# Bias adds on GpSimd, denominators by transposes, and Kronecker inner products on 64x64 blocks with zeros

## What is computed

```python
# L0 and L3, MLP with two biases (the block before is an attention)
y = y + (gelu(norm(y) @ w1 + b1) @ w2 + b2)
# L2 cross-attention and L3 self-attention: softmax in two steps
o = exp(scores) @ v ; out = (o / sum(exp(scores))) @ Wo
# L0 feed-forward: each row goes to 2 of 64 experts, with weights s_k;
# an expert is a sum of Kronecker products, applied to the row as a 32x32 matrix X
h = gelu(sum_k s_k * (B_k.T @ (X @ A_k)) * scale + bias)
```

## Time and profile before

| | us |
|---|---|
| median of 3 runs | 3536.96 (3536.55 to 3546.62) |
| time of the profiled execution | 3511.47 |
| its span, in which all times of the trace are given | 3509.7 |
| PE busy in the span | 3134.8 (89%) |
| DVE, ACT, POOL busy | 1798.4, 1190.6, 958.8 |
| mean granted clock of PE | 0.948 of full speed |

### The profile page before, as it was taken

One profiled execution on the slowest core, in us unless ns is written; L12 is line 12 of the kernel. 1 busy time (PEld: TensorE's weight loads), 2 busy tenths in 40 slices (PEclk: granted clock), 3 DMA queues, 4 the chain that ended last, 5 costly groups with the idle time before them and its releaser, 6 DMA issues. The chain is left out here.

```text
span 3509.7 us, 74620 instructions
## 1 busy us (share of the span) xinstructions
PE 3134.8 (89%) x30164; PEld 2164.7 (62%) x30164; DVE 1798.4 (51%) x4511; ACT 1190.6 (34%) x2326; POOL 958.8 (27%) x794
## 2 busy tenths in 40 slices
PE   8997999999976868889778999789997999989989
PEld 3434555555666764757445555489997885566656
DVE  7897544543233554343676666543333763355543
ACT  1223333323223432312315565322222562244433
POOL 1002433432001100425427778411111210104001
PEclk9998999999989989979889999889998999999999
DMA  4223000000132020635501110178886200021100
GB/s 154 70 72 87 10 13 13 9 9 14 38 56 25 4 53 0 187 100 173 150 25 33 30 31 22 55 277 330 331 328 226 95 2 13 29 72 50 53 14 19
DMA packets 174053, 287.24 MB, mean 82 GB/s; under 512 B 79254, under 2 KB 144331, under 8 KB 164408
## 3 DMA queue, kind: packets, MB, share of 16 engines
q1 hardware_dynamic: 166264, 262.50, 23.8%
q0 software_dynamic: 7488, 20.46, 1.8%
HBM read 244.50 MB, written 28.48 MB: 78 GB/s over the span
## 5 line engine op out<-in xcount | busy, mean ns | idle before, releaser
L2708 PE MATMUL ps<-L_ffn_xsT,arena 128*128 128x128 f32 x2584 | 306.2, 278 | 0.9 <-DVE L_ffn_xsT L2507 0.9
L2708 PEld LDWEIGHTS ps<-L_ffn_xsT,arena 128*128 128x128 f32 x2584 | 298.9, 194 | 3.0 <-DVE L_ffn_xsT L2507 2.6
L842 POOL TENSOR_TENSOR L_xattn_rn<-L_xattn_ss,mhalf 125x16 f32<-125x16 f32 (+1 forms) x64 | 185.8, 2903 | 257.2 <-DVE L_xattn_ss L905 257.2
L162 POOL TENSOR_TENSOR rstd<-nsc,mhalf 112x4 f32<-112x4 f32 (+2 forms) x24 | 39.4, 1641 | 691.0 <-DVE nsc L155 690.1
L3389 POOL TENSOR_TENSOR L_xattn_pT<-L_xattn_pT,L_xattn_keep 125x678 int32<-125x678 int32 x128 | 190.4, 1510 | 70.2 <-ACT L_xattn_pT L3644 70.2
L2606 ACT ACTIVATE L_ffn_silu<-ps,arena 128x128 f32<-128x128 f32 x280 | 102.9, 368 | 269.3 <-PE ps L2708 253.5
L2516 DVE SCALAR_TENSOR_TENSOR L_ffn_hT<-ps,arena,L_ffn_silu 128x128 f32<-128x128 f32 x280 | 98.0, 351 | 155.9 <-ACT L_ffn_silu L2606 155.9
L2385 POOL DMA_INDIRECT L_ffn_rows_out<-L_ffn_ys,L_ffn_dest x78 | 79.8, 1023 | 319.7 <-DVE L_ffn_ys L2525 304.1
L1019 PE MATMUL ps<-arena,L_xattn_cT 128*125 128x512 f32 x384 | 166.1, 592 | 0.0
L723 PE MATMUL ps<-L_attn_prod,arena 128*32 128x448 f32 (+28 forms) x672 | 153.5, 492 | 11.6 <-DVE L_attn_prod L523 9.7
L2721 PE MATMUL ps<-arena,L_ffn_hT 128*128 128x256 f32 x646 | 153.7, 382 | 7.4 <-ACT L_ffn_ys L2615 7.3
(11 more groups left out here) (610 smaller groups left out, 6808.4 us busy)
## 6 DMA issues: line engine op xcount, KB each, us to landing
arena<-in_L_ffn_up SPq DMA_DIRECT2D x35, 2056.0 KB, 8.1
arena<-in_L_ffn_down SPq DMA_DIRECT2D x35, 1152.0 KB, 8.8
L_xattn_ctxT<-in_ctxT SPq DMA_DIRECT2D x48, 375.0 KB, 4.1
arena<-in_L_ffn_up SPq DMA_DIRECT2D x43, 384.0 KB, 4.7
L_attn_a<-L_attn_skew SPq DMA_DIRECT2D x16, 784.0 KB, 5.2
L_xattn_ctx<-in_ctx SPq DMA_DIRECT2D x30, 375.0 KB
arena<-L_xattn_kp SPq DMA_DIRECT2D x64, 93.8 KB, 3.3
L_xattn_mask<-in_mask SPq DMA_DIRECT2D x32, 164.1 KB, 8.3
```

Source lines behind the costliest of these rows:

```text
L842: nc.gpsimd.tensor_tensor(rn[0:r, i], ss[0:r, i], core.mhalf[0:r, 0:H], ALU.pow).then_inc(po_r.step("root", i), 1)
L2708: ins = nc.tensor.matmul(ps[:, 2 + b % 4, half * TS:(half + 1) * TS], self.up(i % WU, k, half * HM + m), xsT[:, i % 2, k], start=(k == 0), ...
```

## The change

Five edits, of which the last only feeds the others.

1. `Mlp`: b2 is loaded into 112 rows, POOL adds it to x, one chunk (112x1024) at a time, and PE's product with the ones is gone. POOL's loop over chunks is written out; the add of chunk c stands behind the power of chunk c + 1. DVE waits for it ahead of its first add to x.
2. `denominators` in `L2Cross` and `L3Self` are 4 transposes of a quarter of o. The 16 numbers stand 32 columns apart in PSUM, and DVE reads them there.
3. `L0Kron.inward` takes both experts at once: for each pair g and each r one product of 64x64 by 64x64, with X twice on the diagonal of the 64x64 input and zeros beside it.
4. The zeros are written by POOL before the loads. Each chunk has a buffer of its own: chunk 0 the second half of h (7168 numbers in each of 128 partitions), chunk 1 `y` (4096) and `xs` (3584). The load of chunk 0 waits for the first memset, that of chunk 1 for all three, and it no longer waits for u0.
5. The bias of L3's MLP is also made in 112 rows, in the stage ahead of it.

```diff
@@ L0Kron.build
+        by_g = lambda t, n: t[:, 0:n * K * I].rearrange("p (g m) -> p g m", g=n)
+        flat_y, flat_xs = core.y[:, :, :].rearrange("p b c -> p (b c)"), self.xs.rearrange("p g n -> p (g n)")
+        YG = NB * D // (K * I)
+        blocks = [[(0, CG, by_g(flat[:, CG * F:2 * CG * F], CG))],
+                  [(0, YG, by_g(flat_y, YG)), (YG, CG, by_g(flat_xs, CG - YG))]]
...
             def load(q):
                 src = x_rows.rearrange("(g r) (i n) -> r i g n", r=2, n=I)
-                for c in range(4):
-                    sp.dma_start(self.xs[c * I:(c + 1) * I], src[c // K][:, q * CG:(q + 1) * CG, :]).then_inc(rows_in[q], DMA)
+                sp.wait_ge(zeroed, 3 if q else 1)
+                for a, b, to in blocks[q]:
+                    for c in range(4):
+                        sp.dma_start(to[c * I:(c + 1) * I, :, c % K * I:(c % K + 1) * I], src[c // K][:, q * CG + a:q * CG + b, :]).then_inc(rows_in[q], DMA)
...
             load(0)
-            sp.wait_ge(pe_t.sem, pe_t.at(first["u0"] + INNER - 1))
             load(1)
...
         def _(pool):
             norm_pool(core, norm)
+            nc.gpsimd.memset(flat[:, CG * F:2 * CG * F], 0.0).then_inc(zeroed, 1)
+            nc.gpsimd.memset(flat_xs, 0.0).then_inc(zeroed, 1)
+            pool.wait_ge(pe_x.sem, pe_x.at(NCH - 1, "xT", KD - 1))
+            pool.wait_ge(rows_out, DMA)
+            nc.gpsimd.memset(flat_y, 0.0).then_inc(zeroed, 1)
...
             def inward(name, q):
...
-                            for c in range(4):
-                                p = slice(c * I, (c + 1) * I)
-                                ins = nc.tensor.matmul(ps[p, even(n) + b, s * F:(s + 1) * F], self.xs[p, g, :], table[p, g, :], start=True, stop=True)
+                            for r in range(2):
+                                p = slice(r * K * I, (r + 1) * K * I)
+                                ins = nc.tensor.matmul(ps[p, even(n) + b, s * F:(s + 1) * F], part[g][p], table[p, g, :], start=True, stop=True)
@@ Mlp.build
         def _(pool):
-            with pool.Fori(0, NCH) as c:
-                ln.pool(pool, ve_n, po, c)
+            ln.pool(pool, ve_n, po, 0)
+            pool.wait_ge(run.arrived, run.loads)
+            for c in range(NCH):
+                if c + 1 < NCH:
+                    ln.pool(pool, ve_n, po, c + 1)
+                x = core.x[0:T, U * c:U * c + U, :]
+                nc.gpsimd.tensor_tensor(x, x, self.b2.unsqueeze(1).to_broadcast([T, U, D]), ALU.add).then_inc(biased, 1)
...
             def outputs(c):
+                dve.wait_ge(biased, c + 1)
+                core.stand(dve)
...
-                                         start=(i == 0), stop=False)
-                    nc.tensor.matmul(ps[0:T, 4 + u, 0:D], core.ones[0:1, 0:T], self.b2, start=False, stop=True).then_inc(pe_o.step("out", u), 1)
+                                               start=(i == 0), stop=(i == HK - 1))
+                    ins.then_inc(pe_o.step("out", u), 1)
@@ L3Self.build (L2Cross alike, with 97 rows and columns in place of 128)
             def denominators(n):
...
-                    ins = nc.tensor.matmul(ps[0:T, 3, j * HQ:(j + 1) * HQ], o[:, n % 3, j * T:(j + 1) * T], core.ident[:, 0:128:Z], start=True, stop=True)
+                    ins = nc.tensor.transpose(ps[0:T, 3, j * 128:(j + 1) * 128], o[:, n % 3, j * T:(j + 1) * T], core.ident[:, :])
```

More of the change, by code:

```diff
@@ L1168, in build @@
         by_scalar = [first[name] + t for name, turns in self.ORDER if name[0] in "tabuwv" for t in range(turns)]
-        norm, lead, folded, rows_out = (core.semaphore(n) for n in ("norm", "lead", "folded", "rows_out"))
+        norm, lead, folded, rows_out, zeroed = (core.semaphore(n) for n in ("norm", "lead", "folded", "rows_out", "zeroed"))
         rows_in = [core.semaphore(f"rows_in{q}") for q in range(CHUNKS)]
@@ L1222, in _ @@
             norm_pool(core, norm)
+            nc.gpsimd.memset(flat[:, CG * F:2 * CG * F], 0.0).then_inc(zeroed, 1)
[3 more added lines that the diff above has]
+            nc.gpsimd.memset(flat_y, 0.0).then_inc(zeroed, 1)
             for q in range(CHUNKS):
+                if q == 0:
+                    pool.wait_ge(pe_t.sem, pe_t.at(first["u0"] + INNER - 1))
                 if q == 1:
-                    pool.wait_ge(rows_out, DMA)
                     pool.wait_ge(pe_t.sem, pe_t.at(first["u1"] + INNER - 1))
@@ L1574, in inward @@
                 table_kept(f"a_up{q}")
-                ten.wait_ge(rows_in[q], 4 * DMA)
+                ten.wait_ge(rows_in[q], 4 * len(blocks[q]) * DMA)
+                part = {g: to[:, g - a, :] for a, b, to in blocks[q] for g in range(a, b)}
                 for t in range(INNER):
@@ L1689, in build @@
         yn, yT, hT = sb("yn", [T, U, D]), sb("yT", [128, KD, N4]), sb("hT", [128, HK, N4])
-        ln, lead = Norm(core, run, "ln"), core.semaphore("lead")
+        ln, lead, biased = Norm(core, run, "ln"), core.semaphore("lead"), core.semaphore("biased")
         pe_t, pe_u, pe_o = Progress(core, "tensor_yT", ("yT", KD)), Progress(core, "tensor_up", ("up", HK)), Progress(core, "tensor_out", "out")
@@ L1799, in narrow @@
                             ten.wait_ge(ac_h.sem, ac_h.at(c, "act", i))
-                        nc.tensor.matmul(ps[0:T, 4 + u, 0:D], hT[:, i, u * T:(u + 1) * T], self.w2[:, i, :],
-                                         start=(i == 0), stop=False)
-                    nc.tensor.matmul(ps[0:T, 4 + u, 0:D], core.ones[0:1, 0:T], self.b2, start=False, stop=True).then_inc(pe_o.step("out", u), 1)
+                        ins = nc.tensor.matmul(ps[0:T, 4 + u, 0:D], hT[:, i, u * T:(u + 1) * T], self.w2[:, i, :],
+                                               start=(i == 0), stop=(i == HK - 1))
+                    ins.then_inc(pe_o.step("out", u), 1)
             turn(0, True)
@@ L1826, in weights @@
         self.b1 = a.load(d["L0_xattn_b1_c"], 128, self.HK)
-        self.b2 = a.load(every(d["L0_xattn_b2"], 1), 1, D)
+        self.b2 = a.load(every(d["L0_xattn_b2"], T), T, D)
         self.gain = a.load(d["L0_xattn_ln2_g_c"], 128, KD)
@@ L3297, in build @@
         sb, v, kT, k = run.sbuf, self.v, self.kT, self.k
+        DR = (HQ - 1) * Z + 1
         xn, xT = sb("xn", [T, 2, D]), sb("xT", [128, 2, KD * T])
@@ L3495, in inverses @@
                     dve.wait_ge(ac_r.sem, ac_r.at(n - 2, "wide"))
-                nc.vector.reciprocal(inverse[:, n % 2], ps[0:T, bank, at:at + H]).then_inc(ve_r.step("inverse"), 1)
+                nc.vector.reciprocal(inverse[:, n % 2].rearrange("p (j h) -> p j h", j=NQ), ps[0:T, bank, at:at + NQ * DR].rearrange("p (j r) -> p j r", j=NQ)[:, :, 0:DR:Z]).then_inc(ve_r.step("inverse"), 1)
             def divided(n, bank):
@@ L3780, in denominators @@
                 for j in range(NQ):
-                    ins = nc.tensor.matmul(ps[0:T, bank, at + j * HQ:at + (j + 1) * HQ], o[:, n % 2, j * T:(j + 1) * T], core.ident[:, 0:128:Z], start=True, stop=True)
+                    ins = nc.tensor.transpose(ps[0:T, bank, at + j * DR:at + (j + 1) * DR], o[0:DR, n % 2, j * T:(j + 1) * T], core.ident[0:DR, 0:DR])
                 ins.then_inc(pe_r.step("den"), 1)
@@ L4589, in inverses @@
                     dve.wait_ge(ac_r.sem, ac_r.at(n - 2, "wide"))
-                nc.vector.reciprocal(inverse[:, n % 2], ps[0:T, 3, 0:H]).then_inc(ve_r.step("inverse"), 1)
+                nc.vector.reciprocal(inverse[:, n % 2], ps[0:T, 3, 0:H * Z:Z]).then_inc(ve_r.step("inverse"), 1)
             def divided(n):
@@ L4929, in flat @@
             return v
-        row = lambda s: flat(s.rearrange("(a n) -> a n", a=1), 1, 0)
+        row = lambda s: flat(every(s, T), T, 0)
         later = lambda s: None
@@ L4938, in weights @@
         self.bf = generated(lambda s: flat(s, 128, 0), col_d_named(col_d, n + "cf"), n + "cf", lambda s: s, False, mix["cf", "b"])
-        self.bm = generated(row, d, n + "cm", lambda s: s, False, mix["cm", "b"][0:1, :])
+        self.bm = generated(row, d, n + "cm", lambda s: s, False, mix["cm", "b"][0:T, :])
         self.items = [self.cf, self.cm, self.bf, self.bm]
```

## The result

| | before | after |
|---|---|---|
| median of the runs | 3536.82 us (3536.55 to 3546.62) | 3476.10 us (3474.65 to 3479.65) |
| ratio | | 0.9823 (95%: 0.9805 to 0.9842) |
| profiled execution, its span | 3511.47, 3509.7 | 3474.65, 3472.8 |

The change takes off 60.7 us; forecast were 39.2, with 3484 to 3513 us as the range. The direction was right and the size was not. The two profiled spans are only 36.9 us apart, which looks like the forecast's sum and isn't: the first experiment shows why.

What follows compares the result with a forecast made beforehand. PE bounds the MLPs and L3's self-attention, its instruction supply the Kronecker inner products. -19.5 - 7 - 24 + 8.7 + 2.6 = -39.2 us, from 3536.96 to 3497.8 us, predicted as 3497.5; range 3484 to 3513 us.

Steps and rivals of the forecast that it cites:

- 4 chunks of 4 batches in two stages are 32 products of 0.61 us: Both MLPs: removing PE's bias products saves 19.5 us, all of it on the path.
- POOL's add and its cover: MLPs: POOL's add of b2 takes 2.4 us a chunk, under some 8 us of cover, cost 0.
- rival D: MLPs: POOL's add holds L254 and stops PE; at 14 us an add the kernel takes 3549 us; chance 0.02.
- 32 times 0.24: L2 cross-attention and L3 self-attention: denominators by transposes save 7.7 us, taken as -7 (bounds -3 and -9).
- Forecast 2 x 12.1: Kronecker stage: two inner products at 14.8 us in place of 26.9 save 24 us (bounds -21 and -26.6).
- The reading of the pause as want of instructions: Kronecker stage: PE pauses 1.81 us because instructions run out, 3.8 us for each 128 records whatever their shape.
- Forecast +8.7 and +2.6: Kronecker stage's start: POOL's memsets hold DVE's L198 for 8.7 us and L1262 (later L1274) for 2.6 us.
- One gets through: Kronecker stage's start: one L198 runs between the first two memsets, the rest follow the second; +8.7 us, 9.1 if none.
- Rival A: Kronecker stage: the memsets hold nobody; -50.5 us, 3486 us; chance 0.14.
- Cost 0 (bound +5): Kronecker stage: the second load, now following the first, delays nothing; at worst +5 us.
- Rival C: Kronecker stage: the second load delays the first or slows the instruction supply; +6 us, 3504 us; chance 0.13.
- The carry of 25.5 us: Whole kernel: the runs' median lies 25.5 us above the profiled execution, carried over to the forecast time.

Runs made afterwards that it cites:

- the first experiment: The kernel before rerun unchanged (3539.78 us, ratio 1.0000), and before with the MLP, denominator or Kronecker edits alone (-27.0, -12.9, -19.2 us).
- b_mlp: Before with only the MLP edits: POOL adds b2, bias product gone in both MLPs; 3512.80 us, 0.9930 of before.
- b_half: Before with each two Kronecker inner products made as one of twice the columns, 448 records for 896; one timed execution 3483.48 us, 27.5 us below before's median.
- a_small: Changed kernel with four 32x32 by 32x64 inner products for a pair again, new buffers, memsets and loads kept; 3470.24 us, 0.9901 of before.
- a_load1: Changed kernel with the second chunk's load back behind the first inner product; 3446.42 us, 0.9824 of before.
- a_twice: Changed kernel with each 64x64 inner product issued twice, 896 records a chunk; one timed execution 3470.98 us, 32.1 us below before's median.

## Why the prediction was off

Two steps failed. The instructions that went were priced by their own rows, or by another stage's, where taking them out gave more: 25 to 27 us for the bias products in place of 19.5, 12.9 to 14.2 for the denominators in place of 7. And what the new buffers and loads do to the rest of the Kronecker stage was put at nothing, where it gave some 7 us. The memsets and the inner products came out as forecast.

**The bias product: place right, size short.** "4 chunks of 4 batches in two stages are 32 products of 0.61 us". Measured -27.0 us by the medians of b_mlp, and 12.6 and 12.4 us in the traces' two stages, 0.78 us each. The step that failed is to price an instruction by its own row. The earlier trace rows held a sign of the rest: L1800's row is 3.62 us long behind the transposes, but 3.71 us behind a bias product. What it would be between two others of its kind, 3.45 us to the next, stood nowhere, but the difference was there to be asked about. Why the short product costs so much no run shows. POOL's add and its cover were as forecast, and rival D is out.

**The denominators: short as well.** "32 times 0.24". In L3 the stage is 4.7 us shorter (means of six traces without and eight with the edit, 200.6 and 195.9): 0.29 us a batch. In L2 it is 9.5 us (431.1 and 421.6). There the transposes are of 97 columns and hold PE for 0.34 us, and a batch takes 24.57 us in place of 24.99; 16 x 0.42 are 6.7 us. I had taken L3's row for both stages, priced the new transposes by those of L4826 (0.48 us, where they hold PE for 0.43 and 0.34), and counted L2 only in part. L3's steady batches, too, are 0.36 us shorter (10.91 in place of 11.27), where the two holds differ by 0.29. Of the other 2.8 us in L2 some lie in single batches: each of the six traces without the edit has one or two of 26.1 us and more, none of the eight with it has one above 24.9. Why, I leave open.

**The inner products: right.** Forecast 2 x 12.1, measured 12.0 and 11.3 (means of the two traces of before and of the changed kernel). The reading of the pause as want of instructions holds (b_half, a_small).

**The memsets: right, one detail by luck.** Forecast +8.7 and +2.6; the rows of L198 and L1274 are 8.6 and 3.2 us longer, and the first inner product is 12.4 us later in its stage. "One gets through" was wrong, none did; that L198's row still met the 8.7 us, and not the 9.1 of that bound, is luck. Over all traces the start is 37.5 to 43.6 us without the early memsets and 49.9 to 54.8 with them. Rival A is out.

**The rest of the stage, taken as nothing.** Between the inner products and behind them the stage is some 7 us shorter (3.9 and 3.0 by the means of two traces each, which differ among themselves by up to 5), and a_small, with the old products, has this too: its stage is longer than before's by 4.9 us although its start is 13.7 us later. Over all traces the two parts are 5 and 3 us shorter. So it comes with edit 4, the new buffers and the loads into them; which of these does it no run separates. "Cost 0 (bound +5)" for the second load had no lower bound: I asked only whether it could harm. Rival C's slower gather is there, 2.4 us by a_load1, but the gather behind the inner product gives it back.

**The carry of 25.5 us: right.** "The runs' median lies 25.5 us above that execution, which I carry over". The profiled execution had the short level of L1's experts, the timed ones, by their times, the long one; on one chip the difference cancels. The prediction had no cause for the 25.5 us. It is the sum that was 21.5 us short, and my bounds were drawn too tightly around each term: all of them at their better ends, -19.5 - 9 - 26.6 us and no hold, are -55.1 us or 3481.9 us, outside the range that I gave and still above 3476.

**The 36.9 us between the two spans** are 60.3 us of savings in the five stages that the change touches, less 30.9 us for the experts of L1, and 9.5 us by which two unchanged stretches ahead of them happened to be quicker (L1's cross-attention 98.2 in place of 102.5 us, the experts' routing 45.6 in place of 50.8), less 2.0 us in all the others. Had I taken the two profiles at their word, I would have called a wrong sum right.

## What to carry to other kernels

Price an instruction on a full engine by the period with and without it, not by its own row: the neighbours' rows hold part of it, and a product of one row by one row cost more than a full one here. Where PE waits for instructions, count instructions and not work; fewer and larger products gained there, and a_twice shows where that ends. Before two profiled spans are subtracted, compare them stage by stage, those first that the change doesn't touch; and put a memset on POOL where DVE has nothing to do in SBUF.

## What was not expected of the hardware

- A closing product of 1x112 by 1x256 costs 0.80 us, one of 128x112 by 128x256 0.43 us.
- A pass of 12 DVE instructions got no turn between two memsets of POOL that follow each other without a wait: the first took 9.05 us, the length of both.
- Loads of 448 KB in small pieces land in 6.2 to 7.0 us where they go to rows 256 bytes apart in one buffer, and in 10.4 to 11.6 us where they go to dense rows in another (medians of all traces).
- 128 records of small products begin every 3.8 us, whether PE takes 3.58 us for them at the lower clock or 2.01 us at the upper one.
- A stage with indirect DMAs and DVE at work (L1's experts) takes 132 to 135 us on some chips and 166 to 168 us on others, with the same program.
